# Attention's projection rescheduled, batch norm inside layer norm, values 17 wide, ones in strips

## The reference, cut to what matters

```python
# _L0_ffn_ref: batch norm ahead of the queries
mu = jnp.mean(x, axis=0); var = jnp.mean(jnp.square(x - mu), axis=0)
xn = (x - mu) * jax.lax.rsqrt(var + BN_EPS) * gamma + beta
# _L0_attn_b_ref: D_C = 64, N_HEADS = 16, D_K = 16
Q = ((x @ W_dq) @ W_uq); c_kv = x @ W_dkv; K = c_kv @ W_uk; V = c_kv @ W_uv
attn = softmax(where(causal, Q K^T / sqrt(D_K), -inf)); out = (attn @ V) @ W_o
```

## Time and profile before

| | us |
|---|---|
| time, median of 3 runs | 3712.21 (3711.64 to 3713.04) |
| the profiled execution | 3711.52 |
| its span, first to last instruction | 3709.7 |
| mean granted TensorE clock (share of 2.4 GHz) | 0.940 |
| busy: TensorE / VectorE / ScalarE / GpSimd | 3226.0 / 2972.4 / 1573.1 / 672.5 |

### The profile page before, as it was taken

One profiled execution on the slowest core, in us unless ns is written; L12 is line 12 of the kernel. 1 busy time (PEld: TensorE's weight loads), 2 busy tenths in 40 slices (PEclk: granted clock), 3 DMA queues, 4 the chain that ended last, 5 costly groups with the idle time before them and its releaser, 6 DMA issues. The chain is left out here.

```text
span 3709.7 us, 76341 instructions
## 1 busy us (share of the span) xinstructions
PE 3226.0 (87%) x29442; PEld 2265.3 (61%) x29442; DVE 2972.4 (80%) x8985; ACT 1573.1 (42%) x2139; POOL 672.5 (18%) x308
## 2 busy tenths in 40 slices
PE   3997479999999985669999999998379999999997
PEld 2886357778787874423333333333257877878786
DVE  5443699999999995478888888881579999999996
ACT  1221244444444431424665666665144444444441
POOL 0000023333333331020000000000013333333333
PEclk6999699999999997879999999999699999999999
DMA  5535500000000002774222122002800000000000
GB/s 177 190 99 148 191 9 10 19 10 19 11 18 18 10 13 78 233 138 70 39 44 40 35 52 51 7 7 75 261 16 10 10 19 10 19 11 18 19 7 15
DMA packets 210446, 206.73 MB, mean 56 GB/s; under 512 B 50422, under 2 KB 186934, under 8 KB 208694
## 3 DMA queue, kind: packets, MB, share of 16 engines
q1 hardware_dynamic: 208182, 200.47, 19.5%
q10 hardware_dynamic: 1920, 1.57, 0.3%
HBM read 129.18 MB, written 72.42 MB: 54 GB/s over the span
## 5 line engine op out<-in xcount | busy, mean ns | idle before, releaser
L509 PE MATMUL f_p_route<-f_x_w,f_y_hot 128*128 128x64 f16 x8192 | 900.5, 194 | 85.1 <-DVE f_weighted L781 73.7
L533 PE MATMUL f_p_out<-f_kout,f_hidden 128*128 128x256 f16 x6144 | 857.2, 274 | 16.6 <-POOL f_hidden L436 15.9
L522 PE MATMUL f_p_hid<-f_xtc,f_kin_t 128*128 128x256 f16 x6144 | 855.3, 273 | 5.8 <-ACT f_hidden L621 5.7
L436 POOL TENSOR_TENSOR f_hidden<-f_weighted,f_hidden 128x1024 f16<-128x1024 f32 x256 | 610.2, 2384 | 1277.4 <-DVE f_x_w L771 1272.9
L1925 DVE TENSOR_REDUCE at_part_max<-at_p_ring 128x1 f32<-128x512 f32 (+3 forms) x1280 | 706.0, 603 | 119.9 <-PE at_p_ring L1794 75.5
L509 PEld LDWEIGHTS f_p_route<-f_x_w,f_y_hot 128*128 128x128 f16 x8192 | 692.7, 98 | 134.2 <-issue 108.5
L533 PEld LDWEIGHTS f_p_out<-f_kout,f_hidden 128*128 128x128 f16 x6144 | 603.1, 98 | 197.1 <-issue 118.6
L1905 ACT ACTIVATE at_prob<-at_p_s 128x1024 f32<-128x1024 f32 (+3 forms) x640 | 546.3, 895 | 388.3 <-PE at_p_s L1846 196.1
L522 PEld LDWEIGHTS f_p_hid<-f_xtc,f_kin_t 128*128 128x128 f16 x6144 | 602.3, 98 | 79.9 <-issue 10.3
L626 ACT CAST f_hidden<-f_weighted 128x1024 f16<-128x1024 f32 x256 | 343.4, 1341 | 587.5 <-DVE f_weighted L781 587.5
L621 ACT ACTIVATE f_hidden<-f_p_hid 128x512 f32<-128x512 f32 x512 | 301.0, 594 | 434.2 <-PE f_p_hid L522 433.5
(11 more groups left out here) (251 smaller groups left out, 3207.1 us busy)
## 6 DMA issues: line engine op xcount, KB each, us to landing
at_q<-qk SPq DMA_DIRECT2D x42, 256.0 KB, 4.5
at_k<-qk SPq DMA_DIRECT2D x42, 256.0 KB, 4.4
f_ln_xin<-x SPq DMA_DIRECT2D x16, 512.0 KB, 6.4
xt<-f_ln_xt SPq DMA_DIRECT2D x32, 256.0 KB, 5.2
f_kin_t<-kin_t SPq DMA_DIRECT2D x8, 1024.0 KB, 8.2
f_kout<-kout_parts SPq DMA_DIRECT2D x8, 1024.0 KB, 7.2
f_xt_in<-xt SPq DMA_DIRECT2D x32, 256.0 KB, 2.8
f_xres<-x SPq DMA_DIRECT2D x32, 256.0 KB, 2.7
```

The lines of the kernel that those rows point to most:

```text
L436: nc.gpsimd.tensor_tensor(lo, weighted[s % WR], hi, ALU.subtract).then_inc(lo_ready, 1)
L509: last = nc.tensor.matmul(p_route[:, t, :], y_hot[:, s % HR, t // PAIR, :, t % PAIR], x_w[:, s % HR, half, t // PAIR, :, t % PAIR], start= ...
L522: last = nc.tensor.matmul(p_hid[g % 2][:, xp % 2, :], kin_t[:, a, dh, xp * P:(xp + 1) * P], xt[slot][:, b, dh, :], start=i % 6 == 0, stop= ...
L533: last = nc.tensor.matmul(p_out[:, u, :], parts[slot][:, xp, u * P:(u + 1) * P, a], kout[:, b, xp, :], start=g == 0 and i == 0, stop=xp == ...
```

## The change

Four edits.

- *Batch norm in layer norm.* `layer_norm_pass` gets three hooks. SP loads chunk 0 and the identity after the stores of block 4; gamma and beta are loaded after the first part of `kin_t`; the scale and shift are formed at the end of VectorE's and ScalarE's streams of the same block. The separate block is gone, and `routed_experts` finds its first loads done.
- *Projection.* Straight code for 16 chunks on all engines; one semaphore a step in place of two (36 become 21); two banks for the compressed product; TensorE makes the compressed product of chunk n+1 ahead of q, k and v of chunk n; ScalarE copies it after the first parts of chunk n; chunks are loaded up to three ahead, the first two before the padded weights. `v` is no longer zeroed.
- *Values 17 wide* (`VC`): 16 values and a one in SBUF, in DRAM and as the weights of the value product, which writes partitions 32h to 32h+16; VectorE zeroes the output bank once.
- *Ones in strips*: 48 memsets of 3 x 512 in place of three of 3 x 8192.

Unused branches (`PAIRED`, `joint`) are removed; they made no instruction.

```diff
@@ -54,7 +54,7 @@
 
 
 def layer_norm_pass(nc, sem, tag, x_dram, xt_dram, ident_dram, feature_stats=None, xln_dram=None,
-                    prefetch=None):
+                    prefetch=None, last_loads=None, last_root=None, last_statistics=None):
...
@@ -122,6 +122,10 @@
             for u in range(LNB):
                 sp.wait_ge(xln_ready, ONE + NBLK - LNB + u + 1)
                 stores(NBLK - LNB + u, u)
+                if last_loads is not None and u == 0:
+
+                    sp.wait_ge(xt_stored[0], ONE + 16 * NK)
+                    last_loads(sp)
...
+            if last_root is not None:
+                last_root(act)
...
+            if last_statistics is not None:
+
+                dve.wait_ge(counted, ONE + NBLK)
+                last_statistics(dve)
...
-            layer_norm_pass(nc, sem, tag + "ln_", x_dram, xt_dram, ident_dram, bn_st, prefetch=load_weights)
 
             gb_loaded, bn_steps = sem(tag + "gb_loaded"), sem(tag + "bn_steps")
             bn_var_ready, bn_root_ready = sem(tag + "bn_var_ready"), sem(tag + "bn_root_ready")
-            block = first.enter_context(nc.Block())
-
-            @block.sync
-            def _(sp):
-                with nc.allow_non_contiguous_dma(reason="512 scalars"):
-                    sp.dma_start(gb[:, 0, :], gamma.rearrange("(h p) -> p h", p=P)).then_inc(gb_loaded, 16)
-                    sp.dma_start(gb[:, 1, :], beta.rearrange("(h p) -> p h", p=P)).then_inc(gb_loaded, 16)
-
-            @block.scalar
-            def _(act):
+
+            def load_first_chunk(sp):
+                sp.dma_start(xt_in[:], xt_dram[0, :, :, :]).then_inc(xt_loaded, 16)
+                sp.dma_start(ident[:], ident_dram).then_inc(consts_loaded, 16)
+
+            def feature_root(act):
                 act.wait_ge(bn_var_ready, ONE + 1)
                 nc.scalar.activation(scale[:], bn_var[:], ACT.Sqrt).then_inc(bn_root_ready, 1)
 
-            @block.vector
-            def _(dve):
+            def feature_scales(dve):
                 chain = Chain(dve, bn_steps)
...
+            def load_ahead(sp, turn, u):
+                load_weights(sp, turn, u)
+                if (turn, u) == (0, 0):
+                    with nc.allow_non_contiguous_dma(reason="512 scalars"):
+                        sp.dma_start(gb[:, 0, :], gamma.rearrange("(h p) -> p h", p=P)).then_inc(gb_loaded, 16)
+                        sp.dma_start(gb[:, 1, :], beta.rearrange("(h p) -> p h", p=P)).then_inc(gb_loaded, 16)
+
+            layer_norm_pass(nc, sem, tag + "ln_", x_dram, xt_dram, ident_dram, bn_st, prefetch=load_ahead,
+                            last_loads=load_first_chunk, last_root=feature_root, last_statistics=feature_scales)
...
-            sp.dma_start(ident[:], ident_dram).then_inc(consts_loaded, 16)
-            load_xt(0)
             load_xt(1)
...
+VC = DK + 1
...
+            load(0)
+            load(1)
             sp.wait_ge(up_zero, ONE + 3)
             sp.dma_start(up["q"][0:DC, :], W_uq).then_inc(weights, 16)
             sp.dma_start(up["k"][DC:P, :], W_uk).then_inc(weights, 16)
             sp.dma_start(up["v"][DC:P, :], W_uv).then_inc(weights, 16)
-            def load(u, c):
-                sp.dma_start(xt[u][:], xt_dram[bass.ds(c, 1), :, :, :].rearrange("c p h t -> (c p) h t")).then_inc(s["xt_loaded"][u], 16)
-
-            def chunk(b, j, u, last=False):
-                n = b * n_it + j
-                if not last:
-
-                    sp.wait_ge(s["c_ready"][u], ONE + n + 1)
-                    load(u, n * 2 + u + 2)
-                sp.wait_ge(s["v_copied"][u], ONE + n + 1)
-                dst = v_dram[bass.ds(b * (NU // BATCH), NU // BATCH), :, bass.ds((j * 2 + u) * 2 * P, 2 * P)].rearrange("g p c -> p g c")
-                sp.dma_start(dst, v[u][:].rearrange("p g t h c -> p g (t h c)")).then_inc(s["stored"][u], 16)
+            load(2)
+            for n in range(NCH):
+                b, j, u = n // per, n % per, n % 2
+                if n + 3 < NCH:
+                    load(n + 3)
+                sp.wait_ge(s["v_copied"], ONE + n + 1)
+                groups = NU // BATCH
+                dst = v_dram[b * groups:(b + 1) * groups, :, j * 2 * HG * VC:(j + 1) * 2 * HG * VC].rearrange("g p c -> p g c")
+                sp.dma_start(dst, v[u][:].rearrange("p g t h c -> p g (t h c)")).then_inc(stored[u], 16)
...
+            def compress(n):
+                pe.wait_ge(xt_loaded[n % 2], ONE + (n // 2 + 1) * 16)
+
+                above(pe, s["c_copied"], n - 1)
+                for h in range(DH):
+                    last = nc.tensor.matmul(p_c[n % 2][:, 0:CH], down[:, h, :], xt[n % 2][:, h, :], start=h == 0, stop=h == DH - 1)
+                last.then_inc(s["c_ready"], 1)
...
+            compress(0)
+            for n in range(NCH):
+                u = n % 2
+                if n + 1 < NCH:
+                    compress(n + 1)
+                pe.wait_ge(s["c_copied"], ONE + n + 1)
...
+            def copy_compressed(n):
+                act.wait_ge(s["c_ready"], ONE + n + 1)
+
+                above(act, s["v_ready"], n - 1)
+                nc.scalar.copy(ct[n % 2][:], p_c[n % 2][:, 0:CH]).then_inc(s["c_copied"], 1)
+
+            act.wait_ge(v_ones, ONE + 2)
+            copy_compressed(0)
+            for n in range(NCH):
+                u = n % 2
+
+                above(act, stored[u], n // 2 * STORES)
+                for name in "qk":
+                    act.wait_ge(s[name + "_ready"], ONE + n + 1)
+                    nc.scalar.mul(parts[name][u][:, 0, :, :], p_up[name][u][:], scale[name]).then_inc(s["first_" + name], 1)
+                if n + 1 < NCH:
+                    copy_compressed(n + 1)
+                act.wait_ge(s["v_ready"], ONE + n + 1)
...
-                if i:
-                    pool.wait_ge(s["ones_set"], ONE + i)
-                else:
+                if i == 0:
                     pool.wait_ge(s["made"], ONE + 3)
-                nc.gpsimd.memset(k[i][KS_ROWS:KS_ROWS + M_ROWS, :, :], 1.0).then_inc(s["ones_set"], 1)
+                for h in range(HG):
+                    for c in range(QB):
+                        last = nc.gpsimd.memset(k[i][KS_ROWS:KS_ROWS + M_ROWS, h, c * BLK:(c + 1) * BLK], 1.0)
+                last.then_inc(s["ones_set"], 1)
...
-                    last = nc.tensor.matmul(p_o[32 * h:32 * h + 32, off:BLK], v[n % SLOTS][:, kt, h, :], prob[g % 2][:, h, off:BLK],
+                    last = nc.tensor.matmul(p_o[32 * h:32 * h + VC, off:BLK], v[n % SLOTS][:, kt, h, :], prob[g % 2][:, h, off:BLK],
...
+            pe.wait_ge(s["p_o_zero"], ONE + 1)
...
+            nc.vector.memset(p_o[:], 0.0).then_inc(s["p_o_zero"], 1)
```

More of the change, by code:

```diff
@@ L1444 @@
 LEAD, CATCH_UP = 0.58, 1.6
-PAIRED, JOINT = False, 2 * P
 def piece_columns(qt, kb):
@@ L1507, in _ @@
[L1507 to L1515 removed]
+                sp.wait_ge(stored[u], ONE + STORES * NCH // 2)
         @block.gpsimd
```

171 lines of the change are left out of this document (63 added, 108 removed).

## The result

| | us |
|---|---|
| changed kernel, median of 4 runs | 3680.8 (3678.67 to 3686.24) |
| kernel before, beside it, median of 4 | 3712.53 (3711.64 to 3713.04) |
| ratio | 0.9917, 95% interval 0.99 to 0.9934 |
| the profiled execution, its span, its mean clock | 3679.11, 3677.3, 0.943 |

The forecast was 3675, from 3659 to 3690: the time lies in the range, 5.8 us above the forecast. Where the time went can be read from first starts of instructions that both traces have. Each line of this table is the time from one such start to the next; the last column has the extremes of that stage over the runs of this document whose code is the same in it as in the changed kernel, or nearly so.

The account below looks back on a forecast made before the run. Stages run serially on one core: TensorE sets attention's pace, a ring of waits the projection's, with DMA next. Terms -18.8 - 0.5 - 10.7 + 0 - 4.7 - 0.3 - 2 = -37.0 from 3711.5 gave 3675, range 3659 to 3690.

Parts of the forecast that it names:

- (a): Both expert stages: batch norm moved into layer norm, its chain hidden, f_xn starting where batch norm started; -18.8 us.
- less 0.2 each for a wait that is seen only after the barrier: Start of both expert stages: deduction from gains of 10.7 and 9.3 us, leaving 19.6.
- (b): Projection start: fewer semaphores at 0.07 us each, first two chunks loaded before padded weights; -0.5 us.
- (c): Projection pace: compressed product a chunk ahead, wait for stores then comes last; 4.3 us a chunk, -10.7 us.
- the ring: Projection: first split of chunk n waits for chunk n-2's five stores to land; 8.3 to 8.9 us for two chunks.
- SP's queue holds: six issues of 0.5 are 3 us of 4.3: Projection: SP's DMA issues for a chunk take 3 us and fit within the 4.3 us a chunk.
- no store binds: Projection rival: landings fall to about 2.6 us, TensorE's 3.5 us a chunk sets the pace; 3664 us, chance 0.08.
- DMA-bound: Projection rival: DMA engines set the pace, 1.33 MB takes 3.9 to 4.65 us a chunk; 3681 us, chance 0.12.
- (d): Straight code in place of loops on five queues: more instructions to fetch; taken as 0, up to +3 us.
- (e): Head of attention: ones in 48 strips, so VectorE's cast no longer waits for a long memset; -4.7 us.
- (f): Values 17 wide: -0.3 us for a first load, -2 us for narrower weight loads in the attention step loop.
- The slower rival: Attention step loop: 17-column value products do not run side by side, about 2.0 us more each; 4325 us, chance 0.05.

Follow-up runs that it names:

- base_first: Changed kernel with semaphore base_ready allocated first of the experts' semaphores, so SP sets it right behind the barrier; median 3675.23 us, ratio 0.9902.
- late_kout: base_first with the last two of four pieces of kout (1 MB each) loaded behind the barrier in both expert stages; median 3673.5 us, ratio 0.9901.
- loads_act: Changed kernel with three buffers for q and k parts and v, and xt loads from chunk 3 on issued by ScalarE; projection 82.30 us, pace 3.98.
- strips_alone: Kernel before with only the ones of k set in 48 strips of 3x512; median 3707.33 us, ratio 0.9992; head of attention 32.76 us.

## Why the prediction was right, and where it was not

(a) *Batch norm in layer norm*, forecast -18.8, measured -13.2. The mechanism held (block gone, chain hidden, nothing awaited from DRAM); the size was wrong by 5.6 us, the largest part of the miss, and outside its bounds. The step that failed is "less 0.2 each for a wait that is seen only after the barrier". I saw the DMA of chunk 0 go and did not ask which wait of ScalarE is next: it was hidden under that load and is `base_ready`, the last but one of some thirty semaphores that SP sets behind the barrier. It was priced for the projection in part (b), 0.07 us each, and not here. That is 3.1 us of the two stages, shown by `base_first`. Most of the rest is the barrier: counted from the first statistics it comes 1.5 us later in each stage (54.7 and 55.0 us on average over the nine runs, 53.2 and 53.5 over the two), where I took 0.4. In the second stage SP issues the last transposed rows 47.95 us after the first statistics in both kernels, so it is their landing that became longer. `late_kout` shows that bytes in front of it set the barrier; that it is the bytes of chunk 0 and the identity is argued only, and 0.33 MB at the 410 GB/s of that stretch are 0.8 us, half of what was measured.

(b) *Projection start*, -0.5, measured: from POOL's first instruction to the first compressed product 7.47 against 8.49, and to the first split 12.5 against 13.3, -0.7. The count of semaphores was right (SP's first load after 1.70 in place of 2.53).

(c) *Projection pace*, -10.7, measured 64.7 against 74.5, -9.8 or 4.38 us a chunk for 4.3. The number was right and the reason not, which is luck. I gave the pace to the wait for `stored` because the arithmetic of landings met it. Taking the ring away gave 0.5 us: the ring (4.38) stood close in front of what the DMA engines and SP's queue together allow (4.22), and the engines alone allow 4.0 to 4.1. "SP's queue holds: six issues of 0.5 are 3 us of 4.3" is the sentence that failed: it took the length of an issue as fixed. Behind unfinished stores an issue lasts longer, up to 1.2 us for the load of `xt`, and six took 4.3, five 4.0. Of the rivals, "no store binds" fell as well: stores did not bind and it was not 3.5. "DMA-bound" named the resource behind it: 3.9 us at 340 GB/s was its lower end, 4.0 to 4.1 is what the engines allow. (Its sum is slightly off: 4.65 us a chunk would give part (c) 5.8 us, not 5.) The prediction's sign for the ring, ScalarE's idle ended by a DMA, was seen and did not tell the ring from full engines, since both end in the same wait.

(d) *Straight code*, 0: no stall to be seen, and TensorE is full at 3.45 us a chunk in the first chunks of `loads_act`.

(e) *Ones in strips*, -4.7, measured -5.0 by `strips_alone`; 48 strips in 22.5 us, 0.52 each, as worked out.

(f) *Values 17 wide*, -2.3. The stage that I priced, the step loop, gave nothing that can be told from its spread of 4 us; the 13 ns are there (95 ns for 109) and lie beside other work. The bytes of v's stores, which only the DMA-bound rival priced, are worth 6.0 in the projection of the changed kernel: 4.73 us a chunk with the old ones. So (c) came to its 4.3 with one error against another: a reason that does not set the pace, and landings taken from a kernel with wide values. The slower rival, 17 columns not side by side, is refuted by 1.05 us for eight products.

The terms by the rows of the runs that have them: -13.2 (a), -11.1 (b, c and v's bytes), -5.0 (e), 0: -29.3, against a difference of medians of 31.7 with some 3 us of spread. The forecast's 37.0 is (a)'s miss and the 2 of (f) above that, 7.7 in all; that the median came out only 5.8 above the forecast is the spread of the other stages, and luck.

## What to carry to other kernels

When a change takes away the last of several waits, list what else the waiting instruction and its engine's first instruction wait for, semaphores' setting included, before the gain is booked. A wait that the profile names shows who came last, not what sets the pace: when several limits are within a tenth of each other, only a run that loosens one of them tells, and a number that fits is no evidence for its reason. A queue that issues without a gap is not by that a limit: take one issue away and see whether the others become longer. Bytes leave time where a DMA-bound stage moves them, not where the tile is used.

## What the runs showed of the hardware that was not expected

- The time that SP needs to issue a DMA is not fixed, and the engines' busy share does not tell it: `xt`'s 256 KB took 0.34 to 0.59 us (median 0.38) in the kernel before, with the engines at a share of 0.96 to 1.11, and up to 1.2 (median 0.88) in the changed one, where SP's issues followed each other closely; a pair of q stores took 0.9 to 1.4, and 1.4 to 2.2 where SP had one issue fewer a chunk to make.
- With all 16 DMA engines at a share of about 1.0 or more in each, the projection's loads and stores moved 301 GB/s from 1515 to 1560 in the changed kernel, 313 with a third buffer, 330 with the input's load on ScalarE's queue, 344 with q and k in runs of 1536 bytes, and the second layer norm 410 to 414 in its last 10 us.
- Stages of unchanged code differ from one execution to the next by up to 4 us in 930 (step loop) and 6 in 60 (output stage), the layer norms by 0.1 in 46.
